# Attention layer kernel: the output weights split in place, half of the heads during the value projection

## The reference, cut to what matters

```
x = x + einsum('bct,bcd->bdt', x, L0_weights[subjects])        # 32 x 32 x 512
q, k, v = x @ Wq.T, x @ Wk.T, x @ Wv.T       # 32 query heads, 8 key heads, D = 128
q, k = rope(rmsnorm(q)), rope(rmsnorm(k))
k_all = concat(k_cache[block_table], k); v_all = concat(v_cache[block_table], v)   # 512 + 32 keys
p = softmax(where(valid, q @ k_all.T * SCALE, -1e30))
x = x + (p @ v_all).reshape(32, 32, 32 * 128) @ Wo.T           # Wo is 512 x 4096
```

## Time and profile before

| | before |
|---|---|
| median of 3 runs | 1070.72 us (1069.49 to 1070.82) |
| the profiled execution's own time | 1069.31 us |
| its span | 1067.5 us |
| phase 1, to the last projection matmul's end | about 351.8 us |
| steps 0 to 31 of phase 2, by `pt_lo` of step 0 and of step 32 | 360.4 to 448.0 us |
| the other 224 steps and the end | from 448.0 us |

### The profile page before, as it was taken

The page is one execution under the profiler, slowest core; times in us unless marked ns, Lnnn a source line. Parts: engine busy times, 40 slices in busy tenths (PEclk is TensorE's granted clock), DMA queues, the critical chain, the costliest instruction groups (busy, mean ns, idle before and its releaser), DMA issues.

```text
span 1067.5 us, 25187 instructions
## 1 busy us (share of the span) xinstructions
PE 1006.8 (94%) x8585; PEld 807.0 (76%) x8585; DVE 775.0 (73%) x1637; ACT 710.4 (67%) x1959; POOL 529.3 (50%) x650
## 2 busy tenths in 40 slices
PE   4899999999889878799999999999999999999998
PEld 2578888887678657668967977977986986896893
DVE  7789999999994668747846855855864884784680
ACT  4898999887852768736745744854863773674570
POOL 5455665567880346624634633542652652463440
PEclk9999999999999999999999999999999999999999
DMA  6789999989979489956983983983985895697440
GB/s 210 245 295 326 342 385 363 382 294 401 365 254 356 152 280 338 308 184 196 325 261 131 334 263 110 348 266 120 338 274 166 268 325 183 209 342 231 144 155 10
DMA packets 203888, 279.72 MB, mean 262 GB/s; under 512 B 26864, under 2 KB 158448, under 8 KB 202224
## 3 DMA queue, kind: packets, MB, share of 16 engines
q1 hardware_dynamic: 185072, 210.86, 59.4%
q0 software_dynamic: 18688, 67.25, 18.3%
HBM read 231.77 MB, written 46.27 MB: 260 GB/s over the span
## 4 chain that ended last, share of the span: by engine, by line
PE 56%; DMA 11%; DVE 11%; SPq 8%; issue 5%; POOL 5%; ACT 4%; ACTq 0%; DVEq 0%; POOLq 0%
PE ps_o L1304 16%; PE ps_proj L1304 15%; PE ps_o L1429 8%; DMA vs<-v_pages,v_row 6%; PE ps_t L1404 5%; SPq L571 5%; PE ps_s L1393 4%; PE ps_s L1397 4%; POOL vs L783 2%; POOL probs L797 2%; DMA kt<-k_pages_t 2%; DMA w_nat<-in_L_cond_Wq 2%; DMA wo_nat<-in_L_cond_Wo 2%; PE ps_rt L1359 2%; DVE rot L1130 2%
## 5 line engine op out<-in xcount | busy, mean ns | idle before, releaser
L797 POOL TENSOR_SCALAR probs<-probs,recip 128x544 f32<-128x544 f32 x256 | 186.2, 727 | 366.2 <-DVE recip L1243 361.3
L1235 DVE CUSTOM_DVE_ANT_0 probs<-ps_s,mask,row_scale 128x544 f32<-128x544 f32 x256 | 200.0, 781 | 164.4 <-PE ps_s L1397 160.8
L925 ACT ACTIVATE probs<-probs,neg_max 128x544 f32<-128x544 f32 x256 | 191.5, 748 | 134.7 <-DVE neg_max L1235 116.1
L1429 PE MATMUL ps_o<-pt_hi,vs 128*128 128x128 f16 x2048 | 213.7, 219 | 3.6 <-DMA vs<-v_pages,v_row 3.6
L932 ACT ACTIVATE pt_hi<-ps_t 128x512 f16<-128x512 f32 x256 | 149.3, 583 | 75.3 <-PE ps_t L1404 75.2
L1429 PE MATMUL ps_o<-pt_lo,vs 128*128 128x128 f16 x1024 | 185.1, 219 | 0.0
L751 POOL TENSOR_TENSOR roped<-rot 128x256 f32<-128x256 f32 x160 | 142.9, 915 | 81.9 <-DVE rot L1122 70.2
L1247 DVE SCALAR_TENSOR_TENSOR pt_lo<-ps_t,pt_hi 128x512 f16<-128x512 f32 x256 | 174.4, 681 | 10.9 <-ACT pt_hi L932 7.6
L1429 PEld LDWEIGHTS ps_o<-pt_hi,vs 128*128 128x128 f16 x2048 | 168.2, 98 | 10.0 <-DMA vs<-v_pages,v_row 5.9
L1304 PE MATMUL ps_proj<-wt_hi,x0t_hi 128*128 128x512 f32 x384 | 158.6, 413 | 8.0 <-DVE x0t_lo L1023 7.3
L1404 PE MATMUL ps_t<-fixed,probs 128*128 128x128 f32 x1024 | 156.3, 275 | 5.5 <-POOL probs L797 4.0
(11 more groups left out here) (147 smaller groups left out, 1693.0 us busy)
## 6 DMA issues: line engine op xcount, KB each, us to landing
kt<-k_pages_t SPq DMA_DIRECT2D x512, 128.0 KB
c_nat<-in_L_cond_k_cache SPq DMA_DIRECT2D x32, 512.0 KB, 6.1
q_t<-stage SPq DMA_DIRECT2D x64, 256.0 KB, 7.1
c_nat<-in_L_cond_v_cache SPq DMA_DIRECT2D x32, 512.0 KB, 7.1
qt<-q_t SPq DMA_DIRECT2D x32, 512.0 KB
w_nat<-in_L_cond_Wq SPq DMA_DIRECT2D x8, 1024.0 KB, 8.9
k_pages_t<-c_stage SPq DMA_DIRECT2D x16, 512.0 KB, 5.8
c_nat<-in_L_cond_Wo SPq DMA_DIRECT2D x16, 512.0 KB, 7.4
```

Source lines behind the costliest of these rows:

```text
L797: pool.tensor_scalar(probs_of(i), probs_of(i), col(recip, i), 1.0, ALU.mult, ALU.mult).then_inc(p_norm, 1)
L925: act.activation(pr, pr, ACT.Exp, bias=col(neg_max, i), scale=-1.0, accum_out=col(row_sum, i)).then_inc(a_exp, 1)
L1235: dve.tensor_tensor_reduce(out=probs_of(i), in0=ps_s[:, score_cols(i):score_cols(i) + KEYS], in1=mask[(i // HK) % 2][:, mask_at(i):mask_at ...
L1429: ins = pe.matmul(ps_o[n % 2][:, jl * P:(jl + 1) * P], v[:, part, :], p[i % NPT][:, c, :], start=jl == 0 and c == 0 and k == 0, stop=False ...
```

## The change

There is one buffer `wo` for the output weights, 35 slots of [2 x 512] fp16 in each partition. A slot has the size of one head in fp32. Head n is loaded as fp32 into slot n + 3, and its high and low part are written to slot n, so a conversion overwrites the fp32 words of head n - 3 and waits until that head has both parts (`wo_done`). Loads take four heads at a time (1 MB), eight in all, and no load waits for a conversion. Five are issued in units 84, 85, 87, 89 and 92, three after phase 1. Heads 0 to 15 are converted in units 87 to 94, two a unit, by ACT and DVE. Heads 16 to 31 are converted in phase 2 in each second step; of these, POOL does the low part of heads 19, 23, 27 and 31, in loop passes 8, 16, 24 and 32, whose `rest` is 6. The gather of the second sequence's values now waits for the end of the projections (`t_proj`, NU) where it waited for the last rotated key (`t_rt`, NN), since `vs1` lies elsewhere.

```diff
-    NWS = 4
+    WO_LEAD, WO_LOAD = 3, 4
...
-            wo_nat = [sb(f"wo_nat{n}", [P, HID]) for n in range(NWS)]
+            wo = sb("wo", [P, HQ + WO_LEAD, 2, HID], F16)
...
+    WO_LOADS = {84: 0, 85: 1, 87: 2, 89: 3, 92: 4}
+    WO_EARLY, WO_EARLY_AT = 16, 87
...
+    def wo_words(first, count):
+
+        return wo[:, first + WO_LEAD:first + WO_LEAD + count].rearrange("p n s f -> p (n s f)").bitcast(F32)
+
+    def early_heads(u):
+
+        first = 2 * (u - WO_EARLY_AT)
+        return (first, first + 1) if 0 <= first < WO_EARLY else ()
+
+    def late_head(i):
+
+        n = WO_EARLY + i // 2
+        return n if i % 2 == 1 and 0 <= i and n < HQ else None
+
     def on_pool(n):
-        return n % 4 == 3
+        return n >= WO_EARLY and n % 4 == 3
...
-            def load_wo(n):
-                before = n - NWS
-                if before >= 0:
-                    sp.wait_ge(a_wohi, before + 1)
-                    if on_pool(before):
-                        sp.wait_ge(p_wolo, by_pool(before + 1))
-                    else:
-                        sp.wait_ge(v_wolo, before + 1 - by_pool(before + 1))
-                sp.dma_start(wo_nat[n % NWS][:], wo_t[:, n, :]).then_inc(d_wo[n % NWS], 16)
+            def load_wo(k):
+                h0 = WO_LOAD * k
+                sp.dma_start(wo_words(h0, WO_LOAD), wo_t[:, h0:h0 + WO_LOAD, :].rearrange("d n f -> d (n f)")
+                             ).then_inc(d_wo[k], 16)
...
-                if WO_AT <= u < WO_AT + NWS:
-                    load_wo(u - WO_AT)
+                if u in WO_LOADS:
+                    wo_scanned(sp)
+                    sp.wait_ge(t_rt, NN)
+                    sp.wait_ge(v_wlo, HPC * (NCK - 1))
+                    load_wo(WO_LOADS[u])
...
+            for k in range(len(WO_LOADS), HQ // WO_LOAD):
+                load_wo(k)
...
-            pool.wait_ge(t_rt, NN)
+            pool.wait_ge(t_proj, NU)
             load_v(1, *range(NCH))
...
-                if 1 <= i <= HQ and on_pool(i - 1):
-                    wo_low(i - 1)
+                if late_head(i - 1) is not None and on_pool(late_head(i - 1)):
+                    wo_low(late_head(i - 1))
...
+            def wo_high(n):
+                act.wait_ge(d_wo[n // WO_LOAD], 16)
+                if n == 0:
+                    act.wait_ge(v_scale, 3)
+                wo_done(act, max(0, n - WO_LEAD + 1))
+                act.activation(wo[:, n, 0, :], wo_words(n, 1), ACT.Copy, scale=scale[:, WS:WS + 1]).then_inc(a_wohi, 1)
...
+                for n in early_heads(u):
+                    wo_high(n)
...
-                if i < HQ:
-                    wo_high(i)
+                if late_head(i) is not None:
+                    wo_high(late_head(i))
```

More of the change, by code:

```diff
@@ L153, in build @@
     roped = [sb(f"roped{i}", [P, HPC, D]) for i in range(NRP)]
+    w_nat = [sb(f"w_nat{i}", [P, KC, CH]) for i in range(2)]
+    wt_hi, wt_lo = [], []
+    for i in range(2):
+        wt_hi.append(sb(f"wt_hi{i}", [P, KC, CH], F32R))
+        wt_lo.append(sb(f"wt_lo{i}", [P, KC, CH], F32R))
     x0t_hi = sb("x0t_hi", [P, KC, NG * P], F32R)
     x0t_lo = sb("x0t_lo", [P, KC, NG * P], F32R)
-    w_nat = [sb(f"w_nat{i}", [P, KC, CH]) for i in range(2)]
-    wt_hi = [sb(f"wt_hi{i}", [P, KC, CH], F32R) for i in range(2)]
-    wt_lo = [sb(f"wt_lo{i}", [P, KC, CH], F32R) for i in range(2)]
     abs_sums = sb("abs_sums", [P, NSUM])
@@ L210, in build @@
     ptn = [sb(f"ptn{i}", [4 * SEQ, 2, P], F16) for i in range(2)]
-    wo_hi = sb("wo_hi", [P, HQ, HID], F16)
-    wo_lo = sb("wo_lo", [P, HQ, HID], F16)
     ot_hi = sb("ot_hi", [P, HQ, GB, SEQ], F16)
@@ L252, in build @@
     d_vn = [sem(f"d_vn{i}") for i in range(2)]
-    d_wo = [sem(f"d_wo{i}") for i in range(NWS)]
+    d_wo = [sem(f"d_wo{k}") for k in range(HQ // WO_LOAD)]
     d_res = [sem(f"d_res{i}") for i in range(2)]
@@ L275, in build @@
     PAGES_AT, XSUM_AT, K_TABLE_AT = 13, 2, 49
-    KEYS_AT, NEXT_KEYS_AT, PREFETCH, WO_AT, NEW_V_AT = 54, 80, 87, 89, 93
+    KEYS_AT, NEXT_KEYS_AT, PREFETCH, NEW_V_AT = 54, 80, 87, 93
+    WO_LOADS = {84: 0, 85: 1, 87: 2, 89: 3, 92: 4}
+    WO_EARLY, WO_EARLY_AT = 16, 87
     TOP_STEP = 3
@@ L466, in col, with wo_done @@
         return tile[:, i % NPR:i % NPR + 1]
+    def wo_words(first, count):
[6 more added lines that the diff above has]
+        return n if i % 2 == 1 and 0 <= i and n < HQ else None
     def on_pool(n):
-        return n % 4 == 3
+        return n >= WO_EARLY and n % 4 == 3
     def by_pool(n):
-        return n // 4
+        return max(0, n - WO_EARLY) // 4
+    def wo_done(eng, n):
+        if n - by_pool(n) > 0:
+            eng.wait_ge(v_wolo, n - by_pool(n))
+        if by_pool(n) > 0:
+            eng.wait_ge(p_wolo, by_pool(n))
     def ot_of(tile, n):
@@ L572, in load_pages, with load_keys @@
                                  ).then_inc(d_kt[s], 16)
-            def load_keys(b, between):
+            def load_keys(b):
                 load_queries(b)
[L576 to L583, removed]
+                load_pages(b, 0, NPP)
             def load_new_v(b):
@@ L689, in _ @@
             sp.wait_ge(d_x0, 16)
+            for k in range(len(WO_LOADS), HQ // WO_LOAD):
+                load_wo(k)
             for b in range(B):
                 if b + 1 < B:
[L692 to L697, removed]
+                    if b >= 1:
+                        load_keys(b + 1)
                     load_new_v(b + 1)
-                    for n in pieces[NPP // 4:] if b >= 1 else ():
-                        load_wo(n)
                 g, rest = divmod(b - 2, GB)
@@ L800, in wo_low @@
                 pool.wait_ge(a_wohi, n + 1)
-                pool.tensor_scalar(wo_nat[n % NWS][:], wo_nat[n % NWS][:], scale[:, WS:WS + 1], 1.0, ALU.mult, ALU.mult
+                pool.tensor_scalar(wo_words(n, 1), wo_words(n, 1), scale[:, WS:WS + 1], 1.0, ALU.mult, ALU.mult
                                    ).then_inc(p_wosc, 1)
-                pool.wait_ge(p_wosc, by_pool(n + 1))
-                pool.tensor_tensor(wo_lo[:, n, :], wo_nat[n % NWS][:], wo_hi[:, n, :], ALU.subtract).then_inc(p_wolo, 1)
+                pool.wait_ge(p_wosc, by_pool(n) + 1)
+                pool.tensor_tensor(wo[:, n, 1, :], wo_words(n, 1), wo[:, n, 0, :], ALU.subtract).then_inc(p_wolo, 1)
             norm(0)
@@ L949, in ot_hi_of @@
                                scale=1.0 / P_SCALE).then_inc(a_othi, 1)
[L951 to L954, removed]
             act.wait_ge(v_moff, 1)
@@ L1053, in weight_sum, with wo_low @@
                 dve.tensor_scalar(w_heads(w_sum, c), w_sum_ps(c), TINY_W, None, ALU.add).then_inc(v_wsum, 1)
+            def wo_low(n):
+                dve.wait_ge(a_wohi, n + 1)
+                dve.scalar_tensor_tensor(wo[:, n, 1, :], wo_words(n, 1), scale[:, WS:WS + 1], wo[:, n, 0, :],
+                                         ALU.mult, ALU.subtract).then_inc(v_wolo, 1)
             dve.wait_ge(d_rowi, 16)
@@ L1159, in _ @@
                                                  ALU.mult, ALU.subtract).then_inc(v_clo, 1)
+                for n in early_heads(u):
+                    wo_low(n)
                 if u == PAGES_AT:
@@ L1261, in ot_lo_of @@
                                          1.0 / P_SCALE, ot_of(ot_hi, n), ALU.mult, ALU.subtract).then_inc(v_otlo, 1)
[L1263 to L1266, removed]
             def add_residual(w):
@@ L1296, in _ @@
                     t_lo(i)
-                if 1 <= i <= HQ and not on_pool(i - 1):
-                    wo_low(i - 1)
+                if late_head(i - 1) is not None and not on_pool(late_head(i - 1)):
+                    wo_low(late_head(i - 1))
         @block.tensor
@@ L1449, in project_out @@
                 if g == 0:
-                    pe.wait_ge(v_wolo, YHEADS * (k + 1) - by_pool(YHEADS * (k + 1)))
-                    pe.wait_ge(p_wolo, by_pool(YHEADS * (k + 1)))
+                    wo_done(pe, YHEADS * (k + 1))
                 w, kk = divmod(k, YWIN)
```

2 lines of the change are left out of this document (1 added, 1 removed).

## The result

| | before | after |
|---|---|---|
| median | 1070.77 us (4 runs, 1069.49 to 1071.94) | 1054.89 us (4 runs, 1053.23 to 1055.56) |
| ratio of the runs, 95% interval | | 0.985 (0.9833 to 0.9867) |
| the profiled execution's time, span | 1069.31, 1067.5 us | 1053.23, 1051.4 us |
| `pt_lo`, step 0 to step 32 | 360.4 to 448.0 us | 361.4 to 430.9 us |

The changed kernel is 1.5% faster. The page's busy times show where this does not come from: every engine does the same work as before within 10 us.

A forecast was written before the change was run, and what follows sets the result against it. PE bounds the kernel except in the 32 conversion steps, slowed by ACT's waits for weights and conversion work. 1069.3 + 1.0 - 19.0 = 1051.3; the runs' median is 1.4 above that execution: 1052.7, said as 1052.5 us, range 1047 to 1061.

The forecast's parts named there:

- The heads in the value units: Units 87 to 94: converting heads 0 to 15 costs nothing under PE if weights are there; late loads cost 1.0 us.
- the stall of PE at unit 91: Value units: load 0 lands at 336.5, so PE gets its bank for unit 91 1.0 us late.
- The late last high part: End of the value units: load 3 lands at 349.6, the last high part ends up to 1.4 us late.
- The landing time: 1 MB weight loads in the value units: land 8.9 us after issue, the median of phase 1's twelve loads.
- The steps: The 32 conversion steps of phase 2: waits gone and fewer conversions save 19.0 us, between 12.7 and 22.2.
- The lower bound: Conversion steps of phase 2: only ACT's waits for weights go, fewer conversions buy nothing, saving 12.7 us.
- the floor: Conversion steps of phase 2: PE allows 2.04 us a step, 65.3 us for the stretch, 22.3 less.
- the last sentence of the prediction: Sign of being wrong: steps near 2.4 us with DVE or ACT always busy, so order, not amount, sets the pace.
- DMA after phase 1: Start of phase 2: DMA nearly idle, 0.27 from 360 to 370 us, takes the 6 us of transfers spilling over.
- The transfers set the pace: Rival, conversion stretch: supply of keys and values is the next bound, total 1058 to 1064 us; chance 0.18.
- POOL's passes: Phase 2: POOL's low parts stand in passes without gathers instead of half ahead of one; counted as nothing.
- The moved gather: Second sequence's gather, behind the last projection: four end at 356.9, just covered before `norm` at 357.03; taken as 0.

The follow-up runs named there:

- the repeat: The changed kernel unaltered, run and profiled again beside the kernel with conversions in the even steps, same chip: 1054.01 us, ratio 0.9825.
- the first experiment: Changed kernel with its loads and buffer, but all 32 heads converted in steps 0 to 31, none in the value units: 1059.53 us, ratio 0.9878.
- Without late conversions: Even-steps kernel without converting heads 16 to 31; their loads stay, the projection reads the first 16 heads twice: 1052.16 us, ratio 0.9809.
- the earlier loads: Changed kernel with the first four weight loads issued in units 83 to 86 instead of 84, 85, 87 and 89: 1053.74 us, ratio 0.9835.
- the experiment: Changed kernel with POOL's low parts those of heads 17, 21, 25, 29, three of the four ahead of a gather: 1056.12 us, ratio 0.9845.

## Why the prediction was right, point by point

The forecast was 1052.5 us in 1047 to 1061; 1054.89 came. For the profiled execution the sum said 1051.3, and it took 1053.23, 1.9 more: 0.9 in the steps and 1.0 behind step 32, while the start came out as said. What it named as signs of being right all came: 69.5 us for the 32 steps, no wait of ACT for weights in them, the first scores at 354.93 us, and PE with the least idle time.

- **The heads in the value units.** That they are covered by PE held: PE is busy 10.00 of 10 us from 330 to 350. That the price of 1.0 us for late loads came out is in part luck. The first `pt_lo` starts at 361.4 against 360.4, but projections that end 0.6 us later are a part of this, and what late loads cost was 1.0 us in this execution and 0.1 in the repeat of the same kernel. Of the term's two parts, the stall of PE at unit 91 did not come: SP had issued load 0 at 325.95 and not at 327.6, and it landed in 8.1 us. The late last high part did come. Load 3 was there at about 350.0, computed 349.6, by two errors that cancel: SP issued it at 339.03 and not at 340.7, and it took 11.0 us and not 8.9.
- **The landing time.** The median of the `w_nat` loads, 8.9 us, was the right row for the middle: 8.1 to 11.0, median 9.5, in the place itself; the bound of 10.0 was passed by the load that mattered. The 6.15 us of the Trainium skill's "DMA: Bandwidth & Descriptors", section Bandwidth, was too short here; the trace does not agree with it for a 1 MB load among other transfers.
- **The steps.** 19.0 us were taken between 12.7 and 22.2; 18.1 came, 0.9 less. The lower bound itself was met by the first experiment (12.5 with the loads). The prediction left 3.3 us between its figure and the floor, because three engines wait for one another; 4.2 were left. It did not see which part of that is order and which amount: the same 16 conversions one step earlier take 65.9 us, 21.7 less than before, so 3.6 us are the order, and more than the missing 0.9. That the order may set the pace stands in the last sentence of the prediction as a sign of being wrong; the steps near 2.4 us that it names with it did not come (2.17). That 19.0 lay so near was a choice between two bounds, and not computed.
- **The floor.** 2.04 us a step was taken as what PE allows. Without late conversions the steps without a wait for keys come to 1.98 (`pt_lo` from 395.9 to 427.6 us in 16 steps), with PE busy 31.70 of 31.70 us. So PE is the floor, as said, and the stage read for it held small waits too (PE 0.7 us for values).
- **DMA after phase 1.** The prediction called it nearly idle from 360 to 370 us and had the late loads issued right after phase 1. It is busy there, 0.71, and SP waits for the stores until 366.49: the last one took 9.1 us to land, where the kernel before took 3.1 for the same store. In the changed kernel little came of it. The next thing to be late are the keys of the third sequence, at step 13: 0.7 us here (the weight loads in PE's queue), 1.6 to 3.9 us in four of the experiments' profiles, 0.6 or less in the others. Whether the late stores cause this is open. SP issues these keys behind them, but with the earlier loads it did so 1.4 us earlier (from 371.62) and they came no earlier, and no run took SP's wait away. "The transfers set the pace" was thus right in one place and wrong for the stretch.
- **Behind step 32** the prediction changed nothing; the rest took 620.5 us in the profile against 619.5. In the repeat it took 1050.5 - 430.4 = 620.1. That 1 us, as far as it is one, is unexplained.
- **POOL's passes** were counted as nothing; by its runs the experiment cannot be told from zero, and in its profile steps 16 to 31 are 1.2 us longer without a wait for `vs`. Here the change's small last part stays open. The moved gather was counted as nothing too; it had 0.9 us to spare in one execution and was 0.5 us late in the repeat.

Not tried: the gather of the second sequence at its old place, since `vs1` lies on space that phase 1 still reads.

## What to carry to other kernels

Take the waits out first and price them by the list of waits: the wait of 12.7 us for weights was worth 12.5, taken out together with the other changes to the loads. When work moves into a stretch where another engine is the limit, the cover holds only if its data are there, and under full queues a load's landing time must be read from loads of that size in the same trace. Work that is inserted in each second step belongs into the step that has no other extra work; which of the two it was decided 3.6 us of the stretch at the same amount.

## What the runs showed of the hardware that was not expected

From 340 to 350 us the transfers ran at 408 GB/s, with 1 MB loads, stores and key pages together, where the kernel before had 358 (it had 408 from 320 to 330 us). The last 256 KB store of phase 1 let SP go on only 9.5 us after its issue, with the DMA share between 0.90 and 0.97; in the kernel before the same store landed 3.1 us after its issue, with a share of 0.73 from 350 to 355 us and 0.25 behind it. PE's wait of 3.6 us for keys in one profile was followed by a granted clock of 0.51 over 5 us; behind the waits of 1.4 us in two others it stayed at 1.00.
